# Counting gates by three additions, spreading the gating over five steps, moving coefficients and last sums, and scaling all rows on ScalarE

## The reference

```
x = x + tanh(g_xattn) * cross_attention(layernorm(x), ctx)      # first block
y = layernorm(x)                                                # second block
q, k = y @ Wq, y @ Wk                       # 8 heads of 64
gl_v, gl_o = y @ Ws, y @ Wd                 # 8 heads x 5 experts each
wv     = top2_mask(gl_v) * sigmoid(gl_v)
v      = sum over experts e of wv[e] * (y @ Wv[e])
attn   = softmax(q @ k.T / 8) @ v
mask_o = top2_mask(gl_o)
x = x + tanh(g_ffn) * sum over heads, experts of mask_o * attn @ Wo[e]
```

## Time and profile before

| | us |
|---|---|
| three runs, median (lowest, highest) | 1344.02 (1339.81, 1344.22) |
| the profiled execution | 1345.36 |
| its span, first to last instruction | 1343.6 |
| TensorE (PE) busy in the span | 1241.4 |
| VectorE (DVE) busy | 863.9 |
| ScalarE (ACT) busy | 633.9 |
| GpSimd (POOL) busy | 661.3 |

### The profile page before, as it was taken

The page is one execution under the profiler, slowest core; times in us unless marked ns, Lnnn a source line. Parts: engine busy times, 40 slices in busy tenths (PEclk is TensorE's granted clock), DMA queues, the critical chain, the costliest instruction groups (busy, mean ns, idle before and its releaser), DMA issues.

```text
span 1343.6 us, 19767 instructions
## 1 busy us (share of the span) xinstructions
PE 1241.4 (92%) x6376; PEld 922.3 (69%) x6376; DVE 863.9 (64%) x1531; ACT 633.9 (47%) x1402; POOL 661.3 (49%) x483
## 2 busy tenths in 40 slices
PE   3899999999999996899799799899899999999996
PEld 2688888888888885767567567477576576576564
DVE  5677777867777662665765765666666666666554
ACT  4343434434343331566545545555554554555551
POOL 2524242434324242492771871871961962952961
PEclk9799999999999998999999999999899899899998
DMA  6231313333131233000010010010020020010010
GB/s 225 73 113 45 117 62 94 94 101 109 47 117 39 86 130 110 32 0 32 1 64 31 0 62 31 0 62 31 0 65 28 0 85 9 0 62 0 8 55 32
DMA packets 40714, 75.73 MB, mean 56 GB/s; under 512 B 3761, under 2 KB 4273, under 8 KB 40689
## 3 DMA queue, kind: packets, MB, share of 16 engines
q1 hardware_dynamic: 40688, 75.42, 17.0%
HBM read 58.63 MB, written 16.78 MB: 56 GB/s over the span
## 4 chain that ended last, share of the span: by engine, by line
PE 35%; DVE 9%; POOL 7%; issue 6%; ACT 3%; DVEq 0%; POOLq 0%; ACTq 0%
PE ps_r L1575 7%; PE ps_s L1635 6%; PE ps_r L1587 5%; PE ps_r L1610 5%; PE ps_o L1648 5%; PE ps_s L1627 4%; POOL v_acc L1163 3%; POOL spare L1157 2%; DVE stage L1331 2%; DVE nmax L1336 2%; PE ps_r L1601 2%; POOL z L1175 2%; DVE coef L1380 1%; DVE beaten L1423 1%; DVE q L1394 1%
## 5 line engine op out<-in xcount | busy, mean ns | idle before, releaser
L1336 DVE TENSOR_REDUCE nmax<-ps_s 128x1 f32<-128x512 f32 x256 | 164.2, 683 | 110.7 <-PE ps_s L1627 109.7
L1214 ACT ACTIVATE probs<-ps_s,nmax 128x512 f32<-128x512 f32 x256 | 174.1, 691 | 92.9 <-DVE nmax L1336 92.9
L1223 ACT ACTIVATE pt<-ps_s 128x512 f32<-128x512 f32 x256 | 140.0, 598 | 138.2 <-PE ps_s L1635 137.9
L1163 POOL TENSOR_TENSOR v_acc<-v_acc,spare 128x512 f32<-128x512 f32 x128 | 180.5, 1410 | 10.0
L1635 PE MATMUL ps_s<-ident,probs 128*128 128x128 f32 x1024 | 146.4, 284 | 41.7 <-ACT probs L1214 41.5
L1175 POOL TENSOR_TENSOR z<-z,z_tmp 128x1280 f32<-128x1280 f32 x40 | 117.0, 2924 | 137.2 <-DVE z_tmp L1356 132.8
L1635 PEld LDWEIGHTS ps_s<-ident,probs 128*128 128x128 f32 x1024 | 111.2, 143 | 93.6 <-ACT probs L1214 56.1
L1157 POOL TENSOR_TENSOR spare<-xv,pick 128x512 f32<-128x512 f32 x128 | 134.4, 1050 | 10.0
L1627 PE MATMUL ps_s<-k,q 64*128 64x512 f32 x768 | 123.8, 427 | 3.8 <-ACT pt L1223 3.8
L1648 PE MATMUL ps_o<-pt,v_acc 128*64 128x512 f32 x512 | 123.8, 628 | 0.7 <-ACT pt L1223 0.7
L226 POOL TENSOR_TENSOR e_t<-e_t 128x512 fp32r<-128x512 f32 x32 | 40.3, 1302 | 149.3 <-ACT e_t L432 149.3
(11 more groups left out here) (166 smaller groups left out, 2212.3 us busy)
## 6 DMA issues: line engine op xcount, KB each, us to landing
stage<-in_x SPq DMA_DIRECT2D x32, 256.0 KB, 3.3
stage<-in_ctx SPq DMA_DIRECT2D x32, 256.0 KB, 2.8
x_sb<-in_x SPq DMA_DIRECT2D x8, 1024.0 KB, 5.3
x_dram<-x_sb SPq DMA_DIRECT2D x32, 256.0 KB, 2.1
stage<-x_dram SPq DMA_DIRECT2D x8, 1024.0 KB, 5.6
spare<-x_dram SPq DMA_DIRECT2D x8, 1024.0 KB, 5.5
out_dram<-spare SPq DMA_DIRECT2D x32, 256.0 KB, 2.1
stage<-in_ctx_t SPq DMA_DIRECT2D x28, 256.0 KB, 2.8
```

The source lines that it names most:

```text
L1163: pool.tensor_tensor(acc, acc, v_tmp[:], ALU.add).then_inc(v_steps, 1)
L1214: act.activation(probs[:, n % BANKS, :], ps_s[:, n % BANKS, :], ACT.Exp, bias=nmax[:, n:n + 1], accum_out=den[:, h, t:t + 1]).then_inc(p_e ...
L1223: act.activation(pt[:, h % 4, :, t * P:(t + 1) * P], ps_s[:, n % BANKS, :].rearrange("p (k t) -> p k t", k=NT), ACT.Copy).then_inc(pt_read ...
L1336: dve.tensor_reduce(nmax[:, n:n + 1], ps_s[:, n % BANKS, :], AX_X, ALU.max, negate=True).then_inc(nmax_ready, 1)
```

## The change

- The count over j is no longer one reduction but three additions in `count_better`: j = 0, 1 plus j = 2, 3 into a new 16-bit buffer `halves` (640 elements a partition), the two halves of that (320), and j = 4 on top into `logits` (320, 32-bit out). Each waits for the one before.
- The inversion has a function of its own, at the end of step 1 as before. The routing (pick and mask) moves from the end of step 1 to the end of step 3.
- Coefficients move from steps 8, 16, 24, 32 to steps 13, 21, 29, 34, place 2 as before.
- The last two sums move one step later each, to step 42 place 1 and step 43 place 0.
- ScalarE scales all four row tiles: 0 and 1 at step -13, 2 and 3 at step -11, behind that step's high halves. VectorE's two operations and the semaphore `y_dve` go; TensorE's turning waits for ScalarE alone.

```diff
--- before.py
+++ after.py
@@ -876,11 +876,13 @@
     RESULT_AT = [[46], [47], [48], [49]]
 
     NORMALISE_AT = -13
+    NORMALISE_TILES = {NORMALISE_AT: (0, 1), NORMALISE_AT + 2: (2, 3)}
     GATES_AT = -1
-    ROUTE_AT = 1
+    ROUTE_AT = 3
 
     MIX_PLACES = [(1, 1), (2, 0)]
-    LAST_SUMS = [(2, 1), (3, 0)]
+    LAST_SUMS = [(3, 1), (4, 0)]
+    COEFFICIENTS_AT = [13, 21, 29, 34]
 
     BANKS = 4
 
@@ -954,6 +956,7 @@
         logits = sb("logits", [P, 2, E, NT * H])
 
         beaten = sb("beaten", [P, 2, E, E, NT * H], BF16)
+        halves = sb("halves", [P, 2 * E, 2, NT * H], BF16)
         pick = sb("pick", [P, 2, E, NT, H])
         sig = sb("sig", [P, E, NT * H])
         coef = sb("coef", [P, H, NT, E])
@@ -992,7 +995,6 @@
         w_lo = {name: sem(name + "_lo") for name in ("wq", "wk", "wx", "wo")}
         norm_ready = sem("norm_ready")
         last_newton = sem("last_newton")
-        y_dve = sem("y_dve")
         y_act = sem("y_act")
         yt_ps = sem("yt_ps")
         yt_hi = sem("yt_hi")
@@ -1077,7 +1079,7 @@
             return slice(a * DH, a * DH + DH)
 
 
-        COMPARISONS, GATES = 2 * (E - 1), 3
+        COMPARISONS, GATES = 2 * (E - 1), 5
 
 
         V_STEPS = 2 * E - 1
@@ -1196,12 +1198,12 @@
                         act.wait_ge(w_loaded[name][k], 16)
                     act.activation(weight_tile(name, 0, k), passing(name, k), ACT.Copy).then_inc(w_hi[name], 1)
 
-            def normalise(b, first):
+            def normalise(b, tiles, first):
                 act.wait_ge(norm_ready, b + 1)
                 if not first:
 
                     act.wait_ge(x1_loaded, b * 16)
-                for t in (2, 3):
+                for t in tiles:
                     act.activation(stage[:, t, :], stage[:, t, :], ACT.Identity, bias=norm[:, 1, t:t + 1],
                                    scale=norm[:, 0, t:t + 1]).then_inc(y_act, 1)
 
@@ -1277,8 +1279,8 @@
                     return
                 for name, i in ended(n):
                     part_hi(b, name, i, first)
-                if n == NORMALISE_AT:
-                    normalise(b, first)
+                if n in NORMALISE_TILES:
+                    normalise(b, NORMALISE_TILES[n], first)
                 if n == GATES_AT:
 
                     act.wait_ge(logits_ready, b * NT + NT)
@@ -1319,17 +1321,8 @@
                 if not first:
 
                     dve.wait_ge(last_newton, ROOT_STEPS + 1)
-                    dve.wait_ge(y_act, b * 2)
+                    dve.wait_ge(y_act, b * NT)
                 dve.tensor_scalar(norm[:], x1_norm[:, :, bass.ds(b * NT, NT)], 1.0, None, ALU.mult).then_inc(norm_ready, 1)
-
-            def normalise(b, first):
-                dve.wait_ge(norm_ready, b + 1)
-                if not first:
-
-                    dve.wait_ge(x1_loaded, b * 16)
-                for t in (0, 1):
-                    dve.tensor_scalar(stage[:, t, :], stage[:, t, :], norm[:, 0, t:t + 1], norm[:, 1, t:t + 1], ALU.mult,
-                                      ALU.add).then_inc(y_dve, 1)
 
             def row_max(b, n):
                 dve.wait_ge(s_ready, b * STEPS + n + 1)
@@ -1425,21 +1418,27 @@
             def count_better(b):
 
                 dve.wait_ge(compared, (b + 1) * COMPARISONS)
+                rows = beaten[:].rearrange("p s k j g -> p (s k) j g")
+                dve.tensor_tensor(halves[:], rows[:, :, 0:2, :], rows[:, :, 2:4, :], ALU.add).then_inc(gates, 1)
+                dve.wait_ge(gates, b * GATES + 1)
+                dve.tensor_tensor(halves[:, :, 0, :], halves[:, :, 0, :], halves[:, :, 1, :], ALU.add).then_inc(gates, 1)
                 dve.wait_ge(sig_exp, b + 1)
-                dve.tensor_reduce(logits[:].rearrange("p s k g -> p (s k) g"),
-                                  beaten[:].rearrange("p s k j g -> p (s k) g j"), AX_X, ALU.add).then_inc(gates, 1)
+                dve.wait_ge(gates, b * GATES + 2)
+                dve.tensor_tensor(logits[:].rearrange("p s k g -> p (s k) g"), halves[:, :, 0, :], rows[:, :, 4, :],
+                                  ALU.add).then_inc(gates, 1)
 
             def count_values(b):
                 dve.tensor_scalar(sig[:], sig[:], 1.0, None, ALU.add).then_inc(gates, 1)
 
+            def invert(b):
+                dve.wait_ge(gates, b * GATES + 4)
+                dve.reciprocal(sig[:], sig[:]).then_inc(gates, 1)
+
             def route_values(b, first):
-                dve.wait_ge(gates, b * GATES + 2)
-                dve.reciprocal(sig[:], sig[:]).then_inc(gates, 1)
+                dve.wait_ge(gates, b * GATES + GATES)
                 if not first:
 
                     dve.wait_ge(v_steps, b * PAIRS * V_STEPS)
-
-                dve.wait_ge(gates, b * GATES + 3)
                 dve.scalar_tensor_tensor(pick[:, 0].rearrange("p e t h -> p e (t h)"), logits[:, 0], 1.5, sig[:],
                                          ALU.is_lt, ALU.mult).then_inc(pick_ready, 1)
                 if not first:
@@ -1466,10 +1465,10 @@
                     if n == GATES_AT + 1:
                         count_better(b)
                         count_values(b)
+                    if n == GATES_AT + 2:
+                        invert(b)
                     if n == ROUTE_AT:
                         route_values(b, first)
-                    if n == NORMALISE_AT:
-                        normalise(b, first)
 
             def spread(b, n, place):
 
@@ -1477,7 +1476,7 @@
                     at = TURN_O_AT[p]
                     if (n, place) == (PAIR * p + PAIR, 0):
                         row_sums(b, p)
-                    if (n, place) == (PAIR * p + PAIR, 2):
+                    if (n, place) == (COEFFICIENTS_AT[p], 2):
                         coefficients(b, p)
 
                     for h, (step_at, place_at) in zip((2 * p, 2 * p + 1), MIX_PLACES):
@@ -1559,7 +1558,7 @@
                 if part == 0:
                     wait_bank(b, (name, n), first, last)
                 if name == "turn_y":
-                    pe.wait_ge(*((y_dve, b * 2 + n + 1) if n < 2 else (y_act, b * 2 + n - 1)))
+                    pe.wait_ge(y_act, b * NT + n + 1)
                     for k in range(ND):
                         end = pe.transpose(ps[:, k * P:(k + 1) * P], stage[:, n, k * P:(k + 1) * P], ident[:])
                     end.then_inc(yt_ps, 1)
```

## The result

| | before | after |
|---|---|---|
| median (lowest, highest), us | 1344.02 (1339.81, 1344.33) | 1350.71 (1348.56, 1353.34) |
| the profiled execution | 1345.36 | 1348.56 |
| its span | 1343.6 | 1346.8 |
| mean granted TensorE clock | 0.970 | 0.961 |

The ratio is 1.006, with a 95% interval of 1.0039 to 1.0082: the changed kernel is slower by 5 to 11 us, inside the predicted range, and 1.6 us above the predicted time.

The account below looks back on a forecast made before the run. The prediction took a loop from pick through GpSimd, VectorE and TensorE to bound the kernel. First batch -2.0, first pick +1.6 and six passes +5.5 made +5.1 on 1344.02, so 1349.1 us, range 1345 to 1355.

Parts of the forecast that it names:

- The loop: Pick, 17.23 of GpSimd, 7.21 of VectorE, then TensorE set the 99.15 pass; a later pick lengthens it equally.
- The rival in which TensorE's stalls at steps 4 and 22 come back in each pass: TensorE's stalls, not GpSimd, set the pass: 2.16 and 0.67 come back, -21, about 1323; chance 0.07.
- The three additions: VectorE's count takes 1.28 (other end 1.78) against 2.92 for the reduction, a gain of 1.64 or 1.14.
- The rival of slow additions: The additions run at the comparisons' rate, seven times 0.50 more: +8.6, so 1352.6; chance 0.17.
- Coefficients: On VectorE, moving them saves nothing at step 8; at steps 13 and 21 it costs 0, at most 1 a pass.
- pick and the 17.23 of GpSimd: Pick comes 1.59 later, behind maxima and k's low half; 17.23 is from pick to GpSimd's add end, before product 7.
- Last sums: VectorE, GpSimd's last add to turn_z: same operations reordered, maxima first, TensorE's step 12 turning about two us earlier, length 7.2.
- The 7.2: VectorE's time from GpSimd's last add to turn_z, taken as unchanged; could be 0.6 less or 1.3 more.
- the clock rival: Two shorter stalls around step 12 keep TensorE at 2.4 GHz: 0.4 a pass gained, +2.3, so 1346.3; chance 0.13.
- The 0.67 at step 22: TensorE's wait before the first experts goes with all rows scaled on ScalarE: -0.67 in each of six passes.
- The ends of the span: First batch: step 4 stall goes, -2.0, and first pick on the loop +1.59; after the last turn_z nothing changes.

Follow-up runs that it names:

- adds_only: The kernel before with only the count changed, from one reduction to three additions: 1331.43 us, ratio 0.9911.
- route_only: The kernel before with only the routing (pick and mask) moved from the end of step 1 to the end of step 3: 1365.1 us, ratio 1.0162.
- pick_early: The changed kernel with pick directly behind the inversion at the end of step 1, the mask staying at step 3: 1327.28 us, ratio 0.9895.
- after_sums_back: The changed kernel with the last two sums back at their old places, step 41 place 1 and step 42 place 0: 1342.31 us, ratio 1.0001.
- after_adds_wait: The changed kernel with GpSimd's adds of heads 4 and 5 ahead of pair 0's values, behind a wait for the three additions: 1288.3 us, ratio 0.9591.
- scale_only: The kernel before with only the scaling changed, all four row tiles on ScalarE: 1335.05 us, ratio 0.9941.
- order: The kernel before with only the coefficients and the last sums moved: 1340.91 us, ratio 0.9992.
- after_again: The changed kernel measured once more, unchanged, for comparison: 1350.74 us, ratio 1.0065.

## Why the prediction was right, and where it missed

**The loop.** Right, and shown four ways: pick 1.65 earlier gave 1.84 a pass (adds_only); 3.20 later gave 3.18 (route_only); 3.11 earlier than in after gave 3.00 (pick_early); and cut altogether, the pass fell to 91.49. The kernel before shows it too. In its last four passes the clock is low once more between steps 4 and 12, and TensorE's work there takes 1.7 longer; the stall at step 12 is 2.08 instead of 3.80, and the pass stays at 99.12 to 99.15. The rival in which TensorE's stalls at steps 4 and 22 come back in each pass is out: both are nearly gone in after, and the pass grew.

**The three additions.** Predicted 1.28, measured 1.28 from 834.41 to 835.69. The 16-bit ones took 0.48 for 640 elements and 0.33 for 320, the third with 32-bit output 0.49 for 320. The rival of slow additions is out. The Trainium skill's VectorE: DVE Perf Modes, section on the perf-mode tier table, gave the first two their double rate, and the trace agrees: the second takes 0.33 where the third, as large but with a 32-bit output, takes 0.49.

**Coefficients.** Those at steps 13, 21 and 29 took 1.14, 2.10 and 2.63 in the pass shown, the one at step 34 took 0.21, and TensorE has no wait behind them: nothing, as predicted.

**pick and the 17.23 of GpSimd.** pick 1.59 later was right to 0.17, and product 7 starts 0.03 after the second add.

**The step that missed: "Last sums" and the stalls behind it.** The 7.2 was right in length (7.13). But I wrote that step 12 would split into about 2 and 2.4. It split into 5.59 and 1.58. From compare to turn_z the loop sets the length (35.97 before, 37.29 after, in the pass shown). So what TensorE no longer loses at step 4, and what pick adds, it must lose at step 12. My own numbers give 3.80 + 2.16 + 1.59, about 7.5, and not 4.4; measured are 7.17. With that the clock rival turns round: it supposed two stalls both shorter than 3.80, and expected a gain of 0.4 a pass. Instead the clock is at 1.2 GHz ahead of turn_z (0.50 for 761 to 767, where before had 0.95 for 762 to 768), and it stays low for 2.7 to 5.9 behind it. after_sums_back prices it: 8.4 us in all, 1.2 a pass from trace to trace (100.17 against 98.97). The price of low clock was mis-sized as well: I took 0.3 or so for turn_z from 2.79 against 2.50, but that last pass is itself at low clock there for 2.1, and at the full clock turn_z takes 1.53 (after_adds_wait).

How the move of the sums brings this about isn't shown. The second idle piece before turn_z suggests itself, but the same two pieces are followed by 2.7 of low clock in one pass of after and by 5.9 in another, and in route_only a single piece of 7.54 is followed by 2.3 to 2.7.

**The 0.67 at step 22.** It went, but it was mis-sized. TensorE's stretch from turn_z to compare is 60.9 wherever a pass has the full clock in it (six of the kernels here have such passes), with or without scaling on VectorE. Before stood 2.27 above that: 0.67 of wait and 1.6 more, most of it low clock. After stands 1.97 above it, all of it low clock. So I should have asked not what the edit takes off the 63.19, but how far TensorE stays from full clock: -0.30 a pass came where I had -0.67.

**Luck in the number.** The -0.30 is itself the sum of two misses that cancel. With the sums back (after_sums_back) the stretch from turn_z to compare takes 61.53, 1.66 less than before, where I had 0.67 less; scale_only alone took 1.55 off it. The move of the sums then puts 1.37 back there (1.20 a pass, with what it gains behind GpSimd's add), where I had nothing. Pick came 1.42 later for 1.59. Without the move of the sums the pass is 98.97, 0.18 below the kernel before, and the ratio is 1.0001: the loop was right, but that the change is slower hangs on the low clock behind turn_z, which the forecast didn't have.

**The ends of the span.** Here too errors of other sign meet. Predicted were -0.4 until the first turn_z, +5.5 for six passes and nothing behind them. The traces show -2.79, +6.1, then +1.74 (the last pass to the seventh turn_z, clock 0.93 against 0.97) and -1.89 (the tail). They sum to +3.2, the difference of the spans. Of the -2.79, 0.93 was there when the attention began (526.06 against 526.99). From the first compare to the second it took 2.63 less (77.97 against 80.60), where I had 2.0. In the tail the same 36 matmuls with Wo follow:

```profile
1325.57:1343.60 18.03, 13.30 (x48) 10.55 (x48) 5.08 (x7) 1.79 (x3) 0.00 (x0) 0.77 0.16 59
```

is before, and after is

```profile
1330.68:1346.80 16.12, 11.37 (x48) 9.06 (x48) 5.08 (x7) 1.79 (x3) 0.00 (x0) 0.89 0.18 66
```

with the same count of matmuls at another clock. The change didn't touch this stretch; no run here separates what moved the clock there. The medians differ by 6.7, which is nearer to the six passes than the spans are.

**The parts together.** Each ratio times 1343: additions -12, scaling -8, order -1, routing +22, in all +1; the change has +8.7 in after_again. The 8 between them is what after_sums_back takes away: alone, the sums' move costs nothing, and with the other parts it costs 8. Where TensorE's idle time around step 12 is shorter, as in pick_early, it costs 4 to 6 (1327.28 against 1323.35, or 0.9895 against 0.9853).

Left open: why the passes of after differ among themselves (101.1, 100.05 and 99.5 in turn, and in after_again the same again), with more or less low clock behind turn_z. The traces show that, not what decides it. Nor was it tried whether the 1.37 before turn_z in after_adds_wait goes with the sums back.

## What to carry to other kernels

When the busiest engine still stalls, follow the loop over all engines and ask at which place in an in-order queue the late input is needed. Work that needs nothing late (here two adds of z) belongs ahead of work that does, but look first at what it will then run beside, since operations may shut each other out. And a stall that an edit removes from a stretch whose length the loop sets turns up again at that engine's next wait: add it there before judging that wait.

## What the runs showed of the hardware

**Who is held by GpSimd.** An addition on VectorE with both operands in SBUF took 2.94 beside GpSimd's add instead of 0.33, pick 1.55 instead of 0.32, the mask (one input) 2.92 instead of 0.24; the reduction over 1600 elements took 3.05 beside such an add, its usual time. The Trainium skill's SBUF — State Buffer, section "Who interferes with whom", says that a VectorE instruction with two SBUF inputs contends with GpSimd's reads, that a tensor_scalar in a two-port mode does too, and that a tensor_reduce never does. The traces agree in all three, though no run shows in which mode the mask ran. The price depends on the holder: the held operations ended 0.1 to 0.2 behind GpSimd's add (925.46 and 925.28, 936.92 and 936.74, 845.75 and 845.64), so an instruction of 0.3 can cost 2.9. That is also a quality of the reduction that its replacement lacks: three additions are faster, but one that meets GpSimd's add is held.

**What low clock costs here.** From turn_z to compare TensorE takes 60.93 at 2.4 GHz. Each us at 1.2 GHz behind turn_z adds 0.45 to 0.48 (after and after_sums_back: 1.2 of it gives 61.48, 5.9 gives 63.81).

**Idle time alone doesn't tell the clock behind it.** 7.52 of idle time in one piece left a granted clock of 0.89 to 0.90 in the 6 us behind turn_z in every pass of after_sums_back, 7.54 in one piece left 0.77 to 0.80 in route_only, and 5.58 and 1.58 left 0.50 to 0.77 in after. The traces don't show what else decides.
